# Values of two row tiles in one matmul, scores in the order 3, 2, 1, 0, layer norms' normalisation on VectorE, and fewer waits

## The reference

```
n   = (x - mean) / sqrt(var + 1e-5)                    # over the last axis
q,k,v = n Qs + Qbs, n Ks + Kbs, n Vs + Vbs             # 16 heads of 64
p   = softmax(causal(q k^T / 8))
x   = x + (p v) O + Ob
f   = the same layer norm of x
x   = x + fp4_linear(silu(fp4_linear(f, w_gate)) * fp4_linear(f, w_up), w_down)   # inner width 352
```

## Time and profile before

| | |
|---|---|
| median of 3 runs | 1259.02 us (1258.76 to 1259.97) |
| profiled execution, first to last instruction | 1256.5 us |
| runs' median less that span | 2.5 us |
| PE matmul busy | 1186.2 us, 94% |
| DVE busy | 1130.9 us, 90% |
| ACT busy | 997.1 us, 79% |
| POOL busy | 858.5 us, 68% |
| mean granted TensorE clock | 0.986 of full speed |
| PE, values (L271) | 5120 records of 128 columns, 309.9 us |
| HBM over the span | 12 GB/s |

### The profile page before, as it was taken

The page is one execution under the profiler, slowest core; times in us unless marked ns, Lnnn a source line. Parts: engine busy times, 40 slices in busy tenths (PEclk is TensorE's granted clock), DMA queues, the critical chain, the costliest instruction groups (busy, mean ns, idle before and its releaser), DMA issues. The chain is left out here.

```text
span 1256.5 us, 35752 instructions
## 1 busy us (share of the span) xinstructions
PE 1186.2 (94%) x9610; PEld 843.2 (67%) x9610; DVE 1130.9 (90%) x3771; ACT 997.1 (79%) x2894; POOL 858.5 (68%) x1379
## 2 busy tenths in 40 slices
PE   5877999999999999999999999999999999999864
PEld 3655676777777677777777677767777777777643
DVE  5899889999999998999999899999999999999867
ACT  6767888888889788888988888798888879888521
POOL 3443557867777786767778676777767677777753
PEclk9999999999999999999999999999999999999887
DMA  4554666666565566656666665556665556656610
GB/s 102 156 135 120 172 156 159 166 155 159 148 159 153 154 163 157 156 143 160 154 161 159 158 157 152 149 158 161 157 164 156 148 149 156 163 149 163 171 30 13
DMA packets 132520, 185.43 MB, mean 148 GB/s; under 512 B 40328, under 2 KB 66784, under 8 KB 132320
## 3 DMA queue, kind: packets, MB, share of 16 engines
q1 hardware_dynamic: 82128, 98.93, 30.5%
q10 hardware_dynamic: 50192, 84.21, 25.9%
HBM read 11.04 MB, written 4.19 MB: 12 GB/s over the span
## 5 line engine op out<-in xcount | busy, mean ns | idle before, releaser
L517 POOL TENSOR_SCALAR sc<-sc,rinv 128x512 f32<-128x512 f32 (+3 forms) x1024 | 536.5, 541 | 337.6 <-DVE rinv L882 334.4
L636 ACT ACTIVATE sc<-sc,negmax 128x512 f32<-128x512 f32 (+3 forms) x1024 | 563.0, 552 | 173.4 <-DVE negmax L871 124.3
L871 DVE CUSTOM_DVE_ANT_0 sc<-bank,mask 128x512 f32<-128x512 f32 (+3 forms) x1024 | 434.8, 485 | 50.4 <-issue 40.4
L255 PE MATMUL bank<-k_sb,q_sb 64*128 64x512 f32 (+3 forms) x2048 | 316.0, 444 | 12.2 <-ACT k_sb L658 5.5
L271 PE MATMUL bank<-pT,v 128*64 128x128 f32 x5120 | 309.9, 276 | 8.0 <-DMA pT<-w_in 6.3
L271 PEld LDWEIGHTS bank<-pT,v 128*64 128x64 f32 x5120 | 279.1, 137 | 51.0 <-issue 46.2
L255 PEld LDWEIGHTS bank<-k_sb,q_sb 64*128 64x128 f32 x2048 | 168.4, 186 | 148.0 <-issue 101.4
L894 DVE STREAM_TRANSPOSE squares<-sc 128x1024 f32<-128x1024 f32 (+1 forms) x192 | 194.7, 1043 | 0.8
L894 DVE STREAM_TRANSPOSE w_in<-sc 128x1024 f32<-128x1024 f32 (+1 forms) x192 | 192.0, 1038 | 2.1 <-POOL sc L517 1.9
L636 ACT ACTIVATION_READ_ACCUMULATOR sc<-sc,negmax 128x1 f32 x1024 | 193.8, 189 | 0.0
L386 PE MATMUL bank<-zT,wo_sb 128*128 128x512 f32 x256 | 131.5, 595 | 0.0
(11 more groups left out here) (123 smaller groups left out, 1668.1 us busy)
## 6 DMA issues: line engine op xcount, KB each, us to landing
pT<-squares SPq DMA_DIRECT2D x512, 80.0 KB, 2.5
pT<-squares ACTq DMA_DIRECT2D x512, 80.0 KB, 2.3
pT<-w_in SPq DMA_DIRECT2D x512, 80.0 KB, 2.4
pT<-w_in ACTq DMA_DIRECT2D x512, 80.0 KB, 2.4
x_in<-ttn_normalized_resid_pre SPq DMA_DIRECT2D x16, 256.0 KB, 3.3
x<-ttn_normalized_resid_pre SPq DMA_DIRECT2D x16, 256.0 KB, 3.4
out_x<-y_out SPq DMA_DIRECT2D x32, 128.0 KB, 2.7
w_in<-in_L_attn_Ks SPq DMA_DIRECT2D x2, 256.0 KB, 5.2
```

Of the source, the lines that this page charges most:

```text
L255: last = nc.tensor.matmul(to[a][:, at:at + m], q_sb[rows, hs % 2, P * i:P * i + P], k_sb[rows, hs % 2, 0:m], start=True, stop=True)
L517: last = nc.gpsimd.tensor_scalar(p, p, rinv[:, h % 2, a, i:i + 1], 1.0, ALU.mult, ALU.mult)
L636: last = nc.scalar.activation(p, p, ACT.Exp, scale=-1.0, bias=negmax[:, he % 2, a, i:i + 1], accum_out=rsum[:, he % 2, a, i:i + 1])
L871: last = nc.vector.tensor_tensor_reduce(out=sc[:, h % 2, a, AT[i]:AT[i] + m], in0=bank_at[f"S{c}{a}", h][:, at:at + m], in1=mask[:, SEQ - ...
```

## The change

Five things are changed. (1) Chunks: tile 0 of the scores moves from chunk 1 to chunk 2, behind tile 1, so that the tiles lie in the order 3, 2, 1, 0. (2) Values: the products of tiles 3 and 2, and of 1 and 0, with one key tile go into one matmul of 256 columns, whose moving operand takes the two tiles' blocks with a step; the tiles lie in the bank, in `zT` and in `attnT` in the order 3, 2, 1, 0, and `fin` reads them so. (3) Both normalisations move to DVE, at the places of the bias steps, as (x - mean) * 1/std with two operands of one value a partition; the bias tiles and their semaphores go. (4) ACT waits for the turns and for values once a slot ahead of its eight moves, not at each. (5) DVE waits for the moves of the pair before in `turn(0)` alone.

```diff
-    CHUNKS = [[(3, 0)], [(2, 0), (0, 384)], [(1, 0)]]
-    CHUNK_AT = [0, 512, 1024]
+    CHUNKS = [[(3, 0)], [(2, 0)], [(1, 0), (0, 256)]]
+    CHUNK_AT = [0, 512, 896]
+    Z_AT = {3: 0, 2: P, 1: 2 * P, 0: 3 * P}
+    VALUES = [((3, 2), 0), ((3, 2), 1), ((3, 2), 2), ((3,), 3), ((1, 0), 0), ((1,), 1)]
...
-                    for i in (3, 2, 0, 1):
-                        for j in range(i + 1):
-                            for a in range(2):
-                                at = 10 * a + AT[i] // P + j
-                                last = nc.tensor.matmul(to[DH * a:DH * a + DH, P * i:P * i + P],
-                                                        v1[:, pv // NPAIR % 2, j, 2 * (pv % NPAIR) + a, :],
-                                                        pT[:, pv % 2, :, at, :],
-                                                        start=(i == 3 and j == 0), stop=(i == 1 and j == i))
+                    for n, (tiles, j) in enumerate(VALUES):
+                        z, m = Z_AT[tiles[0]], P * len(tiles)
+                        step = (AT[tiles[-1]] - AT[tiles[0]]) // P if len(tiles) > 1 else 1
+                        for a in range(2):
+                            at = 10 * a + AT[tiles[0]] // P + j
+                            last = nc.tensor.matmul(to[DH * a:DH * a + DH, z:z + m],
+                                                    v1[:, pv // NPAIR % 2, j, 2 * (pv % NPAIR) + a, :],
+                                                    pT[:, pv % 2, :, at:at + step * (len(tiles) - 1) + 1:step, :].rearrange(
+                                                        "p g b q -> p b g q"),
+                                                    start=(n == 0), stop=(n == len(VALUES) - 1))
...
# ACT: x_norm and f_norm go; moves_due() ahead of the first move holds the waits of all eight
-                    for j in range(NT):
-                        last = nc.scalar.activation(xn[:, j, :], x_in[:, b2 % 2, j, :], ACT.Identity, bias=xbias[:, j:j + 1],
-                                                    scale=xrstd[:, j:j + 1])
...
+                moves_due()
                 move(1, 2)
...
# DVE
-                    if ht > 1:
+                    if ht > 1 and c == 0:
                         for n in range(4):
                             dve.wait_ge(p_moved[ht % 2][n], 4 * 16 * (ht // 2))
-                    lo, hi = CHUNK_AT[c], (512, 1024, PLEN)[c]
+                    lo, hi = CHUNK_AT[c], (512, 896, PLEN)[c]
...
-                def x_bias():
+                def x_norm():
                     dve.wait_ge(x_rstd, b2 + 1)
+                    if b2 > 0:
+                        dve.wait_ge(xt_done, b2)
+                    for j in range(NT):
+                        last = nc.vector.tensor_scalar(xn[:, j, :], x_in[:, b2 % 2, j, :], xmv[:, j, 0:1], xrstd[:, j:j + 1],
+                                                       ALU.subtract, ALU.mult)
...
-                def f_bias():
+                def f_norm():
                     dve.wait_ge(f_rstd, fc + 1)
+                    if fc > 1:
+                        dve.wait_ge(xq_unit, fc - 1)
+                    for j in range(2):
+                        last = nc.vector.tensor_scalar(fn[:, fc % 2, P * j:P * j + P], rows_of(fc)[:, j, :],
+                                                       fmv[:, fc % 2, j, 0:1], frstd[:, fc % 2, j:j + 1],
+                                                       ALU.subtract, ALU.mult)
```

More of the change, by code:

```diff
@@ L80, in preln_block_kernel @@
         xrstd = sb("xrstd", [P, NT])
-        xbias = sb("xbias", [P, NT])
         xn = sb("xn", [P, NT, D])
@@ L104, in preln_block_kernel @@
         frstd = sb("frstd", [P, 2, 2])
-        fbias = sb("fbias", [P, 2, 2])
         fn = sb("fn", [P, 2, 2 * D])
@@ L134, in preln_block_kernel @@
         x_stats, x_rstd, x_normed = sem("x_stats"), sem("x_rstd"), sem("x_normed")
-        x_biased, f_biased = sem("x_biased"), sem("f_biased")
         xt_done, xhi_done, xlo_done = sem("xt_done"), sem("xhi_done"), sem("xlo_done")
@@ L315, in fin @@
                     for j in range(NT):
-                        last = nc.tensor.transpose(to[:, P * j:P * j + P], attnT[:, P * j:P * j + P], ident[:, :])
+                        last = nc.tensor.transpose(to[:, P * j:P * j + P], attnT[:, Z_AT[j]:Z_AT[j] + P], ident[:, :])
                     last.then_inc(fin_done, 1)
@@ L626, in do @@
                 bx, bo = s.due(XT, NB, NPAIR), s.due(FIN + 1, NB, NPAIR)
-                fc, fx, fu, fh = (s.due_duo(v) for v in (FNORM, FXT, FUP, FHT))
-                b2 = s.due(XNORM, NB, NPAIR)
+                fx, fu, fh = (s.due_duo(v) for v in (FXT, FUP, FHT))
                 def exp(c, a):
@@ L735, in take_hq, with moves_due @@
                                          ACT.Copy).then_inc(ht_taken[1], 1)
[L737 to L742, removed]
-                    for j in range(NT):
-                        last = nc.scalar.activation(xn[:, j, :], x_in[:, b2 % 2, j, :], ACT.Identity, bias=xbias[:, j:j + 1],
-                                                    scale=xrstd[:, j:j + 1])
[L746 to L761, removed]
+                def moves_due():
                     if hm is None:
@@ L769, in move @@
                         act.wait_ge(z_done, hm - 1)
+                def move(c, d):
+                    if hm is None:
+                        return
                     g = (c + d) % 4
@@ L793, in do @@
                 move(3, 3)
-                f_norm()
                 queries()
@@ L798, in do @@
                 take_hq()
-                x_norm()
             walk(do)
@@ L880, in invert @@
                     dve.wait_ge(exp_done[c], 2 * (h + 1))
-                    tiles = (slice(3, 4), slice(0, 3, 2), slice(1, 2))[c]
+                    tiles = (slice(3, 4), slice(2, 3), slice(0, 2))[c]
                     nc.vector.reciprocal(rinv[:, h % 2, :, tiles], rsum[:, h % 2, :, tiles]).then_inc(r_done[c], 1)
@@ L914, in x_bias @@
                     dve.wait_ge(x_rstd, b2 + 1)
-                    nc.vector.scalar_tensor_tensor(xbias[:, :], xmv[:, :, 0], -1.0, xrstd[:, :], ALU.mult,
-                                                   ALU.mult).then_inc(x_biased, 1)
+                    if b2 > 0:
[3 more added lines that the diff above has]
+                                                       ALU.subtract, ALU.mult)
+                    last.then_inc(x_normed, 1)
                 def x_low():
@@ L957, in f_bias @@
                     dve.wait_ge(f_rstd, fc + 1)
-                    nc.vector.scalar_tensor_tensor(fbias[:, fc % 2, :], fmv[:, fc % 2, :, 0], -1.0, frstd[:, fc % 2, :],
-                                                   ALU.mult, ALU.mult).then_inc(f_biased, 1)
+                    if fc > 1:
[4 more added lines that the diff above has]
+                                                       ALU.subtract, ALU.mult)
+                    last.then_inc(f_normed, 1)
                 def xq1():
@@ L1113, in do @@
                 invert(0)
-                f_bias()
+                f_norm()
                 hq4()
@@ L1134, in do @@
                 invert(2)
-                x_bias()
+                x_norm()
                 hq_end()
```

## The result

The changed kernel takes 1266.31 us, median of 5 runs (1263.29 to 1269.74), against 1258.82 for the kernel before beside it (1258.68 to 1259.97). The ratio is 1.0052, with a 95% interval of 1.0035 to 1.0069: 6.5 us slower. The forecast was 1256.1, 2.7 us faster, and 1266.31 lies above its range. The two intervals overlap, so the cost is some 4 to 6.5 us; by the second the time would lie inside the forecast's range, with the sign still wrong.

A forecast was written before the change was run, and what follows sets the result against it. PE was taken to bound the steady part. Terms -1.3 - 1.1 - 0.6 + 0.4 + 0.8 + 0.4 - 1.5 = -2.9 us on the 1256.5 span gave 1253.6; the median lies 2.5 above, so 1256.1 against 1259.02, range 1250 to 1265.

The forecast's parts named there:

- the cost of f_norm on DVE: Ahead of turn(0) and the second swiglu1: 0.2 us more than the bias, 0.05 late in each of 15 groups, +0.8 us.
- a rival: Keys late in every group: order costs +2.6, a pitch of 0.18 adds +1.5; sum +2.7, 1261.7 us; chance 0.18.
- the POOL rival: POOL's instructions come between DVE's in f_norm and x_norm through the port lock: +10.6, 1269.6 us; chance 0.15.
- x_norm's half of that rival: Four x_norm instructions each held by POOL take 1.8 instead of 0.5 us, 3 us a run; whole rival's chance 0.15.
- the +0.4 forecast: In the last two duos both f_norms lie in DVE's chain: +0.4 us.
- First x_norms, -1.1 and -0.6: At the start, x_norm on DVE: first lets PE's transposes start earlier, -1.1 us; second leaves a busy ACT, -0.6.
- x_norm in the quantising stretch, +0.4: Where weights are quantised DVE leads and one x_norm lies there: +0.4 us.
- Values, -1.3: Values matmuls on PE: eight fewer pair starts a slot save 0.010 us a slot over 128 slots, -1.3 us.
- The bound of 0.0028 us a start: Values on PE: a pair's start costs at most 0.0028 us, so eight fewer a slot save at most 2.8 us.
- Order and waits, together -1.5: ACT's fewer waits and tile 0's later exponential: 0.26 us lost a group instead of 0.36, -1.5 us over 15 groups.
- take_attn's part: Tile 0's exponential goes behind take_attn, so ACT's keys come 0.39 us later: 0.22 free, 0.17 late.

The follow-up runs named there:

- by the second: A second comparison of the unaltered changed kernel with the kernel before: ratio 1.0035 (1.0021 to 1.0050), 4.4 us slower.
- e5: Kernel before with f_norm alone moved to DVE: ratio 1.0046 (1.0033 to 1.0060), +5.8 us.
- e10: Changed kernel with f_norm on DVE behind swiglu1(1) instead of ahead of turn(0): ratio 0.9979 to the kernel before, -2.6 us.
- e11: Kernel before with both norms on DVE, x_norm without mean and root, f_norm without root; single run for its trace: starts 0.135 and 0.18 us apart.
- e14: Kernel before with f_norm alone moved to DVE, behind swiglu1(1): ratio 1.0002 (0.9990 to 1.0013).
- e6: Kernel before with x_norm alone moved to DVE: ratio 1.0005 (0.9992 to 1.0018), +0.6 us.
- e16: Kernel before with merged values in the old scores order, waits once a slot, x_norm on DVE, f_norm on DVE behind swiglu1(1): ratio 0.9986, -1.8 us.
- e4: Kernel before with tile 0 of the scores in chunk 2 and values of two row tiles in one matmul: ratio 1.0005, +0.6 us.
- e3: Kernel before with tile 0 of the scores moved to chunk 2, nothing else: ratio 1.0019 (1.0011 to 1.0028), +2.4 us.
- e2: Kernel before with ACT's and DVE's waits once a slot, nothing else: ratio 0.9980 (0.9969 to 0.9990), -2.5 us.

## Why the prediction was wrong

**The step that failed: the cost of f_norm on DVE, "Two times 0.13 take the place of 653.04 - 652.98 = 0.06".** The mechanism, the place and the slack were right: it stands ahead of swiglu1, which empties the bank of the next first scores, and 0.13 us were free. The size was wrong. The 0.13 came from a row of an instruction with an immediate, on integers; this one has two operands of one value a partition, and its starts are 0.25 apart. So 0.44 came in where 0.20 was reckoned, and 0.44 - 0.13 = 0.31 is late instead of 0.07 less rounding: phase 5 shows 0.34, in 15 groups 5.1 us instead of 0.8. e5, e10, e11 and e14 show it from four sides. The prediction named a pitch error of 0.05 and priced it at 1.5 us, inside a rival; the bound was too near, since no row of before had this form on DVE, and the range should have had f_norm at twice its cost. This step is 4.3 us of a miss of 7 to 9. With what the runs show for each term the sum is +5.1 for f_norm in the steady part, some +2.5 for the last duos, nothing for the first x_norms, +2 for the quantising stretch, -1.8 to -2.7 for values and nothing for order and waits: +7 to +8, where 4.4 and 6.5 were measured.

**The sign came the POOL rival's way, for a different reason.** Its point of decision was "f_norm together takes over 0.2 us more than f_bias did". f_norm does take over 0.2 more, and yet POOL does not come between its two instructions in the steady part (0.30 behind the first start, the second started at 0.25). x_norm's half of that rival came true almost to the number, 1.86 us for four where 1.8 was reckoned, and cost next to nothing in the steady part (e6). That 0.51 us of idle time and two slots of lead hide it is the prediction's reason, and no run tests it. In two of the last three duos both of f_norm's instructions are held, each by one of POOL's. DVE and POOL of the kernel after, the first of the two:

```profile
1199.41 3.15 DVE L946 TENSOR_SCALAR fn<-x,fmv,frstd 128x128 f32<-128x128 f32 x2 [1.33 <-POOL frstd L510]
```

```profile
1199.35 1.67 POOL L533 TENSOR_TENSOR hq_y<-hq_y,hq_e 128x704 f32<-128x704 f32 x1
1201.10 1.39 POOL L541 TENSOR_TENSOR hq<-hq_y,hq_scale 128x704 f32<-128x704 f32 x1
```

f_bias was held there by one instruction and took 1.64, f_norm is held by two: 3.15 us. From the start of the last scores to the end it is 84.9 to 90.2 us with f_norm on DVE ahead of turn(0) (four traces, e11 left out, mean 87.0) and 82.8 to 86.1 with it on ACT (ten, mean 84.5); the +0.4 forecast was more like +2.5. The ranges overlap, and with f_norm behind swiglu1(1) it is 84.5, 87.7 and 85.2 (e10, e14, e16), so the place is not shown to matter here.

**First x_norms, -1.1 and -0.6: nothing together.** The first gained 0.72, less than 1.1 as the four take 1.11 and not 0.52. The second went the way that the prediction named and priced too low: it held back the row maxima by 1.35 us, on a DVE beside a busy POOL (1.72 for the four). The first group is not shorter in the mean (70.2 us with x_norm on DVE, 69.8 without).

**x_norm in the quantising stretch, +0.4: about +2.** DVE leads there, the four take 1.8 to 1.9 us beside POOL's (e6, the kernel after), PE's wait for the row maxima behind them is longer by 1.3 us in the old order of the scores and by 1.6 in the new (means of the traces), and a stretch at the lower clock comes with it in six of seven traces.

**Values, -1.3: -1.8 by e4 over e3, -2.6 to -2.7 by slots without a wait.** The bound of 0.0028 us a start was near the truth. By the slots 0.020 to 0.021 us for eight starts are 2.5 to 2.6 ns each. The Trainium skill ("TensorE: Matmul & The Clock Gate", Back-to-back issue gap) has 2.5 ns, and these runs agree with it.

**Order and waits, together -1.5: -2.5 for the waits (e2), +2.4 for the order (e3), nothing together.** take_attn's part was as forecast (keys late by 0.39, PE waiting in 12 of 12), take_x's in phase 1 was missed. In the changed kernel f_norm's leaving ACT gives take_x's part back (phase 2 at 7.81), while PE still waits for the keys in phase 4 in 12 of 12 groups; before in 2.

## What to carry over

Price an instruction on its new engine from a row of the same form: type, columns, and which operands are immediates. Where the trace has none, let the range have twice the price. When work moves to an engine that has room on average, look at what stands directly behind it there and who waits for that: 0.44 us ahead of a step that empties PE's bank cost 5 us a run, the same 0.44 behind it nothing (phase 5 of e10 and e14). Before a difference of two traces at the start is read, measure both from the last step that the change does not touch: x_norm's 0.72 us hid behind a start that was 0.73 later. When a step changes sides of an instruction that waits, list all the waits of that engine that it passes, in all phases.

## What the hardware showed unexpectedly

- DVE's tensor_scalar on 128 float32 columns in SBUF: 0.135 us from start to start with two immediates, 0.18 with one operand of one value a partition, 0.25 with two (e11, and the kernel after).
- DVE's series of tensor_scalar beside POOL's, both on SBUF: each of DVE's four ends 0.08 us behind the end of one of POOL's and takes 0.43 to 0.65 us instead of 0.34. Of the 1.86 us, 0.75 are due to POOL (1.11 with POOL idle). POOL's six take 2.76 us beside them and 2.74 before, so the lock named in the prediction is seen on DVE's side alone. In the steady part it costs PE nothing that e6 can tell.
- An issue of one of these DMAs keeps ACT for 0.51 us in the middle and SP for 0.59, and single ones for up to 2.4 and 2.6 (e2). Before, ACT's issues take 0.51 us in the middle whether one of SP's runs beside them or not; in e2 those that lie beside one of SP's for over four fifths take 0.60. Packing ACT's closer (e2) came with more long issues on ACT and fewer on SP, and with a faster kernel. What makes an issue long is not shown.
